# Attention on one Trainium2 core: row maxima transposed before they are split, an add moved ahead of a maximum, a copy moved to ScalarE, denominators moved behind the value products

## The reference

```python
qn = group_norm(x, gn_w, gn_b)
vn = group_norm(qn, gn_w, gn_b)
q, k, v = conv1x1(qn, wq, bq), conv1x1(vn, wk, bk), conv1x1(vn, wv, bv)
...
attn = softmax(einsum('bhnd,bhmd->bhnm', q, k) * scale, axis=-1)
out = einsum('bhnm,bhmd->bhnd', attn, v)
out = conv1x1(out, wo, bo)
return (out + q_in) / sqrt(2.0)
```

## Time and profile before

| | |
|---|---|
| time, median of 3 runs | 5409.26 us (5408.44 to 5410.91) |
| the profiled execution, its own time | 5410.59 us |
| its span in the trace | 5408.7 us |
| TensorE busy, share of the span | 95% |
| VectorE, GpSimd, ScalarE | 75%, 57%, 51% |
| attention: transposition of the first to that of the last unit | 439.4 to 3960.6 us |

### The profile page before, as it was taken

How to read it: one execution, slowest core, us unless ns; L and a number is a source line. 1 busy time by engine, 2 the same in 40 slices (tenths; PEclk the granted TensorE clock), 3 DMA queues, 4 the chain that set the end, 5 groups by cost and what they waited for, 6 DMA issues and landing times. The chain is left out here.

```text
span 5408.7 us, 98815 instructions
## 1 busy us (share of the span) xinstructions
PE 5157.6 (95%) x31976; PEld 2506.7 (46%) x31976; DVE 4045.6 (75%) x5266; ACT 2747.3 (51%) x5088; POOL 3102.1 (57%) x1336
## 2 busy tenths in 40 slices
PE   6989999999999999999999999999978999999887
PEld 3434444444444444444444444444426555555433
DVE  3228888888888888888888888888845877687633
ACT  1114666666666666666666656666651334434402
POOL 0005888888888888888888888888870000000000
PEclk9998999999999999999999999999989999999998
DMA  3230010000000000000000000001112010000254
GB/s 150 93 124 10 11 27 23 14 25 13 26 23 16 23 13 26 23 15 23 15 24 25 14 23 21 17 25 45 40 64 84 5 35 24 31 17 29 70 164 159
DMA packets 97199, 217.28 MB, mean 40 GB/s; under 512 B 12848, under 2 KB 22192, under 8 KB 93616
## 3 DMA queue, kind: packets, MB, share of 16 engines
q1 hardware_dynamic: 96816, 211.85, 12.4%
HBM read 131.07 MB, written 80.22 MB: 39 GB/s over the span
## 5 line engine op out<-in xcount | busy, mean ns | idle before, releaser
L662 DVE TENSOR_REDUCE b_mx<-b_pmax 128x1 f32<-128x512 f32 x4096 | 2567.2, 682 | 530.1 <-PE b_pmax L518 525.7
L639 ACT ACTIVATE b_prob<-b_pscore 128x512 f32<-128x512 f32 x4096 | 2155.0, 602 | 1323.3 <-PE b_pscore L532 1314.6
L498 POOL TENSOR_TENSOR b_sums<-b_sums,b_prob 128x1024 f32<-128x1024 f32 x1024 | 2441.8, 2385 | 524.5 <-DVE b_sums L687 358.7
L518 PE MATMUL b_pmax<-b_kst,b_qst 96*128 96x512 f32 x4096 | 1772.8, 436 | 50.7 <-DVE b_mx L662 29.0
L532 PE MATMUL b_pscore<-b_qst,b_kst 98*128 98x512 f32 x4096 | 1658.3, 406 | 15.9 <-issue 9.7
L518 PEld LDWEIGHTS b_pmax<-b_kst,b_qst 96*128 96x128 f32 x4096 | 779.7, 190 | 1122.2 <-DVE b_mx L662 983.6
L545 PE MATMUL b_pout<-b_prob,b_vst 128*32 128x512 f32 x8192 | 1093.5, 606 | 0.0
L532 PEld LDWEIGHTS b_pscore<-b_qst,b_kst 98*128 98x128 f32 x4096 | 777.7, 190 | 391.6 <-issue 226.0
L492 POOL TENSOR_TENSOR b_sums<-b_prob 128x1024 f32<-128x1024 f32 x256 | 611.4, 2388 | 452.5 <-ACT b_prob L639 447.3
L1308 DVE SCALAR_TENSOR_TENSOR d_dsum<-d_ypad,d_dw,d_dsum 128x2048 f32<-128x2048 f32 x288 | 682.1, 2368 | 10.2
L1091 POOL TENSOR_TENSOR d_num_w<-d_vks,d_mask 128x128 f32<-128x128 f32 x8 | 3.6, 454 | 762.9 <-ACT d_vks L1269 762.9
(11 more groups left out here) (130 smaller groups left out, 2380.6 us busy)
## 6 DMA issues: line engine op xcount, KB each, us to landing
b_kst<-scratch_kh SPq DMA_DIRECT2D x32, 512.0 KB, 9.2
b_qst<-scratch_qh SPq DMA_DIRECT2D x128, 128.0 KB, 2.5
scratch_att<-b_outn SPq DMA_DIRECT2D x128, 128.0 KB
scratch_num<-d_num SPq DMA_DIRECT2D x64, 256.0 KB, 2.0
f_num<-scratch_num SPq DMA_DIRECT2D x8, 2048.0 KB, 10.1
f_rden<-scratch_rden SPq DMA_DIRECT2D x64, 256.0 KB, 9.5
a_x<-in_x SPq DMA_DIRECT2D x4, 2048.0 KB, 14.6
scratch_qh<-a_high SPq DMA_DIRECT2D x8, 1024.0 KB, 4.0
```

The source lines that it names most:

```text
L498: pool.tensor_tensor(acc, acc, p[:, step, :], ALU.add).then_inc(pool_added, 1)
L518: pe.matmul(pmax[max_bank(place_of(u, m))][:], qst[0:SUMS, b, t * P:(t + 1) * P], kst[0:SUMS, par, j * BANK:(j + 1) * BANK], start=True, s ...
L639: act.activation(prob[:, kt % PBUF, half * BANK:(half + 1) * BANK], pscore[score_bank(hs)][:], ACT.Exp, scale=SCALE).then_inc(exped, 1)
L662: dve.tensor_reduce(mx[:, t, j:j + 1], pmax[max_bank(place_of(u, m))][:], AX.X, ALU.max).then_inc(max_read, 1)
```

## The change

The change has four parts, all in the attention stage.

1. The maxima are transposed unsplit. VectorE makes `mtop` (`top`), TensorE transposes this 128 x 8 tile, ScalarE copies the negated 8 x 128 result into `mhigh`, rounded to F32R (`high_shift`), and VectorE makes `mlow`, the rest, from the same PSUM bank and `mhigh` (`low_shift`, one `scalar_tensor_tensor`), behind the first maximum of pair 15. SyncE waits for `mlow` and sends both rows. `mx` is double-buffered, and the semaphores of the chain are new (`top_ready`, `turned`, `shift_high`, `shift_low`).
2. In the last pair of an octet VectorE's `add` comes ahead of the fourth maximum in place of behind it.
3. `copy_v` moves from VectorE (pair 1) to ScalarE (behind key block 12, so in pair 6).
4. In the last pair of an octet TensorE's `denominators` comes directly behind `times_v`, ahead of the fourth max product.

```diff
-        mx = sb("b_mx", [P, QT, CHUNKS])
+        mx = sb("b_mx", [P, 2, QT, CHUNKS])
-        mneg = sb("b_mneg", [P, 2 * QT])
-        mrow = sb("b_mrow", [2 * QT, P], F32R)
+        mhigh = sb("b_mhigh", [QT, P], F32R)
+        mlow = sb("b_mlow", [QT, P], F32R)
...
+        def bank_free(eng, u, m):
+            here = place_of(u, m)
+            there = here - back(max_bank, here, SLOTS)
...
+            elif there == T_AT:
+                eng.wait_ge(shift_low, done(u))
+            elif there < 0:
+                eng.wait_ge(max_read, maxima(u * MAXES + there + 1))
+            else:
+                eng.wait_ge(max_read, maxima(u * MAXES + (there if there < T_AT else there - 1) + 1))
...
             def load_shift(u, b):
-                sp.wait_ge(max_read, done(transposed_slot(u) + 1))
-                for half in range(2):
+                sp.wait_ge(shift_low, done(u + 1))
+                for half, row in ((0, mhigh), (1, mlow)):
...
             def transpose_shift(u):
-                pe.wait_ge(packed, done(u + 1))
+                pe.wait_ge(top_ready, done(u + 1))
                 if not is_unit(u, ALL - 1):
-                    pe.wait_ge(max_read, done(transposed_slot(u) - back(max_bank, T_AT, SLOTS) + 1))
-                pe.transpose(pmax[max_bank(T_AT)][0:2 * QT, 0:P], mneg[:], ident[:]).then_inc(max_mm, 1)
+                    pe.wait_ge(max_read, maxima((u + 1) * MAXES + T_AT - 3 + 1))
+                pe.transpose(pmax[max_bank(T_AT)][0:QT, 0:P], mtop[:], ident[:]).then_inc(turned, 1)
...
-                        for m in products[3:]:
-                            max_product(u + ahead, m, t_par, t_buf)
-                        if pair == PAIRS - EARLY and not (final and place == TURN - 1):
-                            transpose_shift(u + 1)
                         if pair % (OCT // 2) == OCT // 2 - 1:
                             o = pair // (OCT // 2)
                             if o:
                                 denominators(u, o - 1)
                             elif behind:
                                 denominators(u - 1, OCTS - 1)
+                        for m in products[3:]:
+                            max_product(u + ahead, m, t_par, t_buf)
+                        if pair == PAIRS - EARLY and not (final and place == TURN - 1):
+                            transpose_shift(u + 1)
...
+            def high_shift(u):
+                act.wait_ge(turned, done(u + 1))
+                act.wait_ge(shift_in, done(u * 32))
+                act.activation(mhigh[:], pmax[max_bank(T_AT)][0:QT, 0:P], ACT.Copy,
+                               scale=-1.0).then_inc(shift_high, 1)
+            def copy_v(head, par):
+                act.activation(vst[:, par, :, :], v_tok[:, :, bass.ds(head * HD, HD)],
+                               ACT.Copy).then_inc(v_in, 1)
...
+                    if values and kt == OCT + 4:
+                        act.wait_ge(times_v_done, done(head * UNITS * PAIRS))
+                        copy_v(head + 1, 1 - par)
+                    if shift and kt == 2 * (PAIRS - EARLY) + 1:
+                        high_shift(u + 1)
...
-            def pack_shift(u):
-                dve.wait_ge(max_read, done(slot_of(u, MAXES - 1) + 1))
-                dve.tensor_reduce(mtop[:], mx[:], AX.X, ALU.max).then_inc(mlink, 1)
-                small(u, 1)
-                dve.wait_ge(max_mm, done(u * SLOTS + T_AT + 1))
-                dve.tensor_scalar(mneg[:, 0:QT].bitcast(F32R), mtop[:], -1.0, None, ALU.mult).then_inc(mlink, 1)
-                small(u, 2)
-                dve.scalar_tensor_tensor(mneg[:, QT:2 * QT], mtop[:], -1.0, mneg[:, 0:QT], ALU.mult,
-                                         ALU.subtract).then_inc(packed, 1)
+            def top(u, b):
+                dve.wait_ge(max_read, maxima((u + 1) * MAXES))
+                dve.wait_ge(turned, done(u))
+                dve.tensor_reduce(mtop[:], mx[:, b], AX.X, ALU.max).then_inc(top_ready, 1)
+            def low_shift(u):
+                dve.wait_ge(shift_high, done(u + 1))
                 dve.wait_ge(shift_in, done(u * 32))
-                dve.tensor_copy(mrow[:], pmax[max_bank(T_AT)][0:2 * QT, 0:P]).then_inc(max_read, 1)
+                dve.scalar_tensor_tensor(mlow[:], pmax[max_bank(T_AT)][0:QT, 0:P], -1.0, mhigh[:].bitcast(F32),
+                                         ALU.mult, ALU.subtract).then_inc(shift_low, 1)
...
-                        if pair == PAIRS - EARLY and not (final and place == TURN - 1):
-                            pack_shift(u + 1)
-                        for m in products:
-                            read_max(u + ahead, m)
-                        if pair == PAIRS - EARLY and not (final and place == TURN - 1):
-                            copy_shift(u + 1)
-                        if pair % (OCT // 2) == OCT // 2 - 1:
-                            o = pair // (OCT // 2)
-                            add(u * OCTS + o, o % 2)
-                        if c == 1 and pair == 1 and not (final and par == HEADS_PER_TURN - 1):
-                            dve.wait_ge(times_v_done, done(head * UNITS * PAIRS))
-                            copy_v(head + 1, 1 - par)
+                        shift = not (final and place == TURN - 1)
+                        if pair == PAIRS - EARLY and shift:
+                            top(u + 1, (place + 1) % 2)
+                        for n in range(PER_PAIR):
+                            if n == PER_PAIR - 1 and pair % (OCT // 2) == OCT // 2 - 1:
+                                o = pair // (OCT // 2)
+                                add(u * OCTS + o, o % 2)
+                            if products:
+                                read_max(u + ahead, products[n], (place + ahead) % 2)
+                            if n == 0 and pair == PAIRS - EARLY + 1 and shift:
+                                low_shift(u + 1)
```

More of the change, by code:

```diff
@@ L310, in stage_attention @@
     SLOTS = MAXES + 1
+    MAX_CREDIT = 16 * MAXES
     HEADS_PER_TURN = 2
@@ L360, in stage_attention @@
         max_read = sem("b_max_read")
-        mlink = sem("b_mlink")
-        packed = sem("b_packed")
+        top_ready = sem("b_top_ready")
+        turned = sem("b_turned")
+        shift_high = sem("b_shift_high")
+        shift_low = sem("b_shift_low")
         out_read = sem("b_out_read")
@@ L387, in place_of, with maxima @@
             return m if m < T_AT and not is_unit(u, 0) else m + 1
[L389 to L393, removed]
+        def bank_free(eng, u, m):
+            here = place_of(u, m)
+            there = here - back(max_bank, here, SLOTS)
+            if is_unit(u, 0):
+                if m >= 3:
+                    eng.wait_ge(max_read, maxima(m - 2))
+            elif there == T_AT:
[4 more added lines that the diff above has]
+                eng.wait_ge(max_read, maxima(u * MAXES + (there if there < T_AT else there - 1) + 1))
+        def maxima(n):
+            return n + MAX_CREDIT
         def is_unit(u, n):
@@ L411, in _ @@
             for s in counted:
[L413 removed]
+                sp.sem_inc(s, MAX_CREDIT if s in (max_mm, max_read) else CREDIT)
             sp.dma_start(ident[:], ident_d).then_inc(consts, 16)
@@ L425, in load_shift @@
             def load_shift(u, b):
-                sp.wait_ge(max_read, done(transposed_slot(u) + 1))
-                for half in range(2):
+                sp.wait_ge(shift_low, done(u + 1))
+                for half, row in ((0, mhigh), (1, mlow)):
                     sp.dma_start(qst[SUMS + half:SUMS + half + 1, b, :].bitcast(F32).rearrange(
                         "o (t j) -> o t j", j=P),
-                        mrow[half * QT:(half + 1) * QT, :].bitcast(F32)).then_inc(shift_in, 16)
+                        row[:].bitcast(F32)).then_inc(shift_in, 16)
             def store(u, head, c):
@@ L515, in max_product @@
                 t, j = m // CHUNKS, m % CHUNKS
-                pe.wait_ge(max_read, done(slot_of(u, m) - back(max_bank, place_of(u, m), SLOTS) + 1))
+                bank_free(pe, u, m)
                 pe.matmul(pmax[max_bank(place_of(u, m))][:], qst[0:SUMS, b, t * P:(t + 1) * P],
@@ L626, in read_den, with unit @@
                 act.activation(outd[:], pden[:], ACT.Copy).then_inc(den_read, 1)
-            def unit(u, behind):
+            def high_shift(u):
[6 more added lines that the diff above has]
+                               ACT.Copy).then_inc(v_in, 1)
+            def unit(u, head, par, c, behind, values, shift):
                 for kt in range(KT):
@@ L645, in unit, with turn @@
                         read_den(u - 1)
-            unit(0, False)
-            with act.Fori(1, ALL) as u:
-                unit(u, True)
+                    if values and kt == OCT + 4:
[3 more added lines that the diff above has]
+                        high_shift(u + 1)
+            def turn(i, first, final):
+                for u, head, par, c in units(i):
+                    place = par * UNITS + c
```

(24 more changed lines are left out.)

4 lines of the change are left out of this document (1 added, 3 removed).

## The result

The changed kernel takes 5333.92 us (median of 4 runs, 5324.87 to 5345.51), the kernel before in the same comparison 5409.05 us: ratio 0.9858, interval 0.9846 to 0.9871. It is faster by 75 us where 100 us were forecast. The profiled execution took 5333.46 us, with a span of 5331.6 us. TensorE's granted clock is the same in the mean, 0.983 of full speed before and 0.982 after.

A forecast was written before the change was run, and what follows sets the result against it. TensorE was taken to bound the kernel before, GpSimd after: 4 x 13.56 = 54.24 us plus 0.06 gives 54.3 us a unit; 63 x (55.89 - 54.3) = 100 us off 5410.6 gives 5310 us, range 5295 to 5330 (0.48).

The forecast's parts named there:

- GpSimd takes over as the bound: Attention unit: GpSimd's four octets of 13.56 us, 54.24 us, exceed TensorE's 53.9 us; with 0.06 us allowed, 54.3 us.
- TensorE works there: Pairs without denominators, kernel before: TensorE's starts follow without a hole, 3.06 us a pair, so it works rather than waits.
- Denominators behind the values: TensorE from `times_v` to the next pair's first max product: 2.46 us for 2.72, gaining 0.26 us an octet.
- The split leaves VectorE: Pairs 14 and 15: TensorE gains 0.62 us, then stalls 0.46 us; next unit starts at 2009.97, not 2010.73.
- The add ahead of the maximum: Octet's last pair: costs nothing up to some 0.7 us of waiting; a whole add's wait would stall TensorE 1.7 us.
- The short steps: Small instructions such as VectorE's `mlow` in pair 15, priced at 0.27 us with no wait for GpSimd.
- ScalarE's copy: Values copied on ScalarE: 1.03 us, hidden in its idle time; TensorE loses 1.6 us fifteen times less; unhidden, 15 us in all.
- 63 x (55.89 - 54.3): Whole attention stage: mean unit before less forecast unit, times 63, a gain of 100 us.
- The row comes late: Rival at the next unit's start: the shift row lands late, 1.1 us giving 55.0 us a unit, 5354 us; chance 0.16.

The follow-up runs named there:

- an add less: Changed kernel with GpSimd's last add of each octet left out, so one key block in eight is missing from the denominators: 5278.41 us, ratio 0.9743.
- wide adds: Changed kernel with GpSimd's five adds an octet made in three instructions, one of 1024 columns and two of 2048: 5287.76 us, ratio 0.9757.
- both orders: Kernel before with denominators behind the values and VectorE's add ahead of the fourth maximum; split and copy stay on VectorE: 5343.13 us, ratio 0.9866.
- beside the wide adds: Kernel before with both orders and GpSimd's five adds an octet in three instructions; split and copies stay on VectorE: 5611.77 us, ratio 1.0349.

## Why the prediction was right, and where it was not

**GpSimd takes over as the bound: right.** Forecast 54.3 us a unit, measured 54.37 us; octets 13.56 us forecast, 13.58 us measured. This was no luck: the prediction let VectorE's add wait 0.4, 0.9 and 1.2 us in a unit's first three octets and recover in the last, and the adds take 1.64, 2.09, 2.23 and 1.52 us in the median, where one that waits for nobody takes 1.21 us. Three runs show that GpSimd is the bound: an add less gave 53.48 us, so did the same adds in fewer instructions, and freeing TensorE of its stall gave nothing until GpSimd had room.

**It was nearly the bound before.** The prediction had that (54.24 against 55.50 us) and did not use it; it read the 55.50 us as TensorE's own work ("TensorE works there"). In the quick pace of the kernel with the add's place alone TensorE does the same work in the same order in 54.46 us, so it had room. An octet without its wait for VectorE is 13.56 - 1.16 = 12.40 us. Four of them, 49.6 us, and the four waits for VectorE make the unit: before 3 x 1.16 + 2.33, 55.4 us; denominators' order alone 3 x 1.16 + 3.19, 56.3 us; changed 4 x 1.16, 54.2 us. Measured: 55.51, 56.38 and 54.37 us. The gain lies in one wait of GpSimd, in the unit's last octet: it is 1.17 us shorter, the unit 1.14 us. The sum is bookkeeping, for GpSimd idles for nothing else; that the add's place shortens the wait is shown by the run that puts it back.

**"Denominators behind the values ... a gain of 0.26 us an octet": right for TensorE (0.29 us), wrong as a gain.** By itself the move costs 94 us. The prediction priced it at a gain of nothing to 0.4 us an octet, by TensorE's steps alone.

**"The split leaves VectorE": TensorE's steps came as forecast** (pair 15 begins 1.35 us behind `times_v` of pair 14, forecast 1.50; from there to the next unit 4.56 us, forecast 4.62), but they were hidden: with the split left in place the unit is the same. TensorE by itself was put at 53.9 us a unit, 0.4 us too high: with an add left out, or with wide adds, it runs at 53.48 us.

**The add ahead of the maximum: mis-sized at "cost nothing".** In the changed kernel it carries most of the gain: putting it back costs 0.95 us a unit, of 1.14. Alone on the kernel before it makes it slower (ratio 1.0100), for the split then comes at a bad moment in many units.

**The short steps were right.** `mlow` took 0.27 us, as priced, with GpSimd's adds running. The Trainium skill's rule (SBUF — State Buffer, Who interferes with whom), that an instruction with one SBUF input, outside VectorE's two-port modes, does not meet GpSimd, agrees with all 64 of them: 267 to 279 ns, 63 of them beside a running GpSimd add. ScalarE's copy took 1.06 us (forecast 1.03), with no longer unit for it:

```profile
2054.18 1.06 ACT L652 ACTIVATE b_vst<-v_tok 128x1024 f32 x1
2055.12 2.23 ACT L666 ACTIVATE b_prob<-b_pscore 128x512 f32<-128x512 f32 x4
```

**Most of the 25 us that are missing come from the base of the sum.** It took the mean of 55.89 us and put all of its 0.39 us over 55.50 down to the copies. Units with a copy cost 0.84 us, not 1.6: 0.2 us a unit. The rest, 12 us, are long intervals at the ends of turns, which the change does not touch; so "63 x (55.89 - 54.3)" counted a gain that could not come. Another 4 us are 54.37 for 54.3, and 7 us are late rows.

**The row comes late: in part.** At the starts of some units, most of them the last of a turn, TensorE waits for the row of shifts; the long intervals that these make come to 7 us. TensorE's timeline, a late row and the next unit's start, at the end of a turn:

```profile
2143.33 0.49 PE L548 MATMUL b_pscore<-b_qst,b_kst 98*128 98x512 f32 x1 [0.94 <-DMA b_qst<-b_mlow]
```

```profile
2199.23 0.50 PE L548 MATMUL b_pscore<-b_qst,b_kst 98*128 98x512 f32 x1 [1.70 <-issue]
```

Where the low half is made first, the intervals ahead of a turn's end are of the usual length, so the margin was what was short there. The traces point to what delays the row. In the eight units of the changed kernel (the first aside) whose row is 0.4 us or more late, a packet of 16 KB on a DMA queue that the profile lists as "instruction" begins 2.1 to 2.5 us ahead of the late product, with the row under way; where one begins 0.8 to 1.7 us ahead, the row is in time, and so it is in the one unit where one begins 2.6 us ahead. At five turn starts, too, such a packet begins 2.7 to 3.3 us ahead of the late product. It would fit both that the row and TensorE wait for these transfers, but no run varied them. Two of the long intervals (56.96 and 58.01 us) hold a stretch of 3.4 us at the lower clock besides. Why the changed kernel's runs lie 20 us apart, where those of before lay within 3 us beside them (12 us in another comparison), stays open; ScalarE's long loop body, the one cause tried, is not it.

## What to carry to other kernels

When two engines share work and each shuts the other out, add up the waits of the slower one over a whole period: as long as that engine idles for nothing else, the sum shows which wait makes the period long. TensorE's savings did not show it here. Before an instruction is moved, list what stands behind it on the engine that reads its result; a move that is right for one queue can be worth minus 94 us until the next queue moves with it. Take the base of a sum from undisturbed periods, and account for each long one separately. Look at the granted clock of the slow periods before a wait is given all of their length.

## What the runs showed of the hardware that was not expected

VectorE's short instructions wait for GpSimd's running add by very different amounts as their phase shifts: the high half of the split lasted 1352 ns in the mean before, 457 ns with both orders, 2017 ns beside the wide adds. Where it slipped in at 0.17 us, with the add's place alone, the low half behind it could take up to 2.39 us. One kernel ran at two paces by this (54.46 and 57.8 us a unit), and some 1.5 us of the slower one go with 3.4 us at the lower granted clock. And an add of 2048 columns on GpSimd takes 4.58 us against 2 x 2.38 us, besides the gap of 0.17 us that it saves.
